# Second layer of a two-layer graph network: the base rows reach the node rows by an adding transfer on GpSimd's queue

## What is computed

```python
h = jnp.maximum(_layernorm(x, axis=-1), 0.0)                 # done by the first layer's code
w = relu(edge_length_embedded @ W_fc1 / sqrt(10)) * sqrt(2) @ W_fc2 / sqrt(100)
si0, si1 = (h0 @ W_si0, h1 @ W_si1) * a                      # "base rows", one per node
y0, y1 = (h0 @ W_l1_0, h1 @ W_l1_1) * a  gathered by edge_src
m0..m3 = products of w, y and edge_attr                      # per edge
s0..s3 = segment_sum(m0..m3, edge_dst)                       # per node
out = concat(si0 + 0.5 * (s0 @ W_l2_00 + s3 @ W_l2_10) * a, si1 + 0.5 * (...) * a)
x = x + out
```

## Time and profile before

| what | value |
|---|---|
| median of 3 runs | 2910.91 us (2899.09 to 2930.3) |
| the profiled execution | 2901.78 us, of which the span from first to last instruction is 2900.0 us |
| busy over the span | PE 91%, PEld 84%, DVE 88%, ACT 72%, POOL 61% |
| mean granted TensorE clock | 0.97 of full speed |
| chain that ended last | PE 29% of the span, an unknown queue 3%, every other part 1% or less |

### The profile page before, as it was taken

How to read it: one execution, slowest core, us unless ns; L and a number is a source line. 1 busy time by engine, 2 the same in 40 slices (tenths; PEclk the granted TensorE clock), 3 DMA queues, 4 the chain that set the end, 5 groups by cost and what they waited for, 6 DMA issues and landing times. The chain is left out here.

```text
span 2900.0 us, 93514 instructions
## 1 busy us (share of the span) xinstructions
PE 2652.8 (91%) x26822; PEld 2448.7 (84%) x26822; DVE 2546.0 (88%) x11404; ACT 2101.9 (72%) x5020; POOL 1783.5 (61%) x2035
## 2 busy tenths in 40 slices
PE   0699999999999999999999995799999999999997
PEld 0699999999999999999999994688888888888886
DVE  6799999999999999999999992587888888788886
ACT  1599999999999999999999994354455555444453
POOL 3677766776666677766676661555566555555651
PEclk9999999999999999999999997799999999899998
DMA  5244444444444444444444431455555555455552
GB/s 133 71 108 112 110 111 110 111 111 112 111 108 110 108 114 111 110 112 111 110 111 108 110 100 51 105 144 129 132 146 141 147 142 141 125 141 136 140 140 74
DMA packets 563778, 337.76 MB, mean 116 GB/s; under 512 B 220529, under 2 KB 545684, under 8 KB 563141
## 3 DMA queue, kind: packets, MB, share of 16 engines
q1 hardware_dynamic: 462033, 216.02, 29.4%
q0 software_dynamic: 48736, 83.76, 11.6%
q10 hardware_dynamic: 52500, 32.01, 3.8%
HBM read 199.48 MB, written 132.08 MB: 114 GB/s over the span
## 5 line engine op out<-in xcount | busy, mean ns | idle before, releaser
L677 POOL DMA_INDIRECT xg<-sources,win x501 | 583.8, 1165 | 489.8 <-issue 221.0
L677 POOL DMA_INDIRECT xg<-in_x,win x501 | 611.2, 1220 | 164.8 <-issue 153.2
L1140 PE MATMUL out_ps<-w_out,aggT 128*100 128x64 f32 (+2 forms) x6012 | 635.6, 256 | 9.5 <-issue 6.9
L1140 PEld LDWEIGHTS out_ps<-w_out,aggT 128*100 128x100 f32 x6012 | 607.3, 171 | 12.2 <-issue 7.5
L1128 PE MATMUL agg_ps<-sel,msg 128*128 128x100 f32 x4512 | 594.8, 282 | 6.7 <-DVE msg L824 4.5
L1128 PEld LDWEIGHTS agg_ps<-sel,msg 128*128 128x128 f32 x4512 | 544.2, 195 | 26.3 <-DVE msg L824 5.5
L967 ACT COPY xw_sb<-xw_ps 128x704 f32<-128x704 f32 (+1 forms) x502 | 307.0, 611 | 315.5 <-PE xw_ps L1116 154.0
L1116 PE MATMUL xw_ps<-w_fc,hid 65*128 65x192 f32 (+1 forms) x2004 | 461.2, 354 | 17.9 <-ACT hid L942 13.4
L986 ACT COPY aggT<-agg_ps 128x600 f32<-128x600 f32 x377 | 248.2, 658 | 150.7 <-PE agg_ps L1128 91.0
L1116 PEld LDWEIGHTS xw_ps<-w_fc,hid 65*128 65x128 f32 (+1 forms) x2004 | 322.4, 194 | 33.7 <-ACT hid L942 17.6
L950 ACT ACTIVATE hn<-xn,nmr,rs 128x192 f32<-128x192 f32 x501 | 244.4, 538 | 56.5 <-DVE nmr L772 56.5
(11 more groups left out here) (147 smaller groups left out, 5488.8 us busy)
## 6 DMA issues: line engine op xcount, KB each, us to landing
sources<-ev SPq DMA_DIRECT2D x250, 250.0 KB
xn<-in_x SPq DMA_DIRECT2D x250, 125.0 KB
xmid<-xo SPq DMA_DIRECT2D x250, 125.0 KB
xo<-xmid SPq DMA_DIRECT2D x250, 125.0 KB
xn<-sources SPq DMA_DIRECT2D x250, 125.0 KB
out<-xo ACTq DMA_DIRECT2D x250, 125.0 KB
win<-edge_rec SPq DMA_DIRECT2D x1002, 3.5 KB
ee_sb<-ee_parts SPq DMA_DIRECT2D x501, 18.0 KB
```

Of the source, the lines that this page charges most:

```text
L677: pool.indirect_dma_start(out=xg[:, t.slot, j, 0:D], out_offset=None, in_=edge_rows, in_offset=bass.IndirectOffsetOnAxis(ap=win[:, t.slot, ...
L1140: ins = pe.matmul(rows[0:NT, j, c0:c1], aggT[:, t.half, j, k, :], w[f"out{k}_"][:, :], start=fresh, stop=True, skip_group_check=not fresh)
```

## The change

The addition of the base rows leaves VectorE. GpSimd issues, for each turn, a transfer that reads the base rows from `sources` in DRAM and adds them to what stands in `xo` (`accum_op=ALU.add`). It stands in GpSimd's step behind the gathers, for turn s - 2 in step s, and waits for the landing of the node rows (`xn_in`) and for `rows_ready` of the turn four before it. SP's load of the base rows into `xn` (L626) and VectorE's `add_base` are gone. One semaphore becomes four used in turn, and a fifth for the serial pass. In the serial pass GpSimd reads the tile's number itself, adds, waits for the landing, and only then gathers.

```diff
-    base_added = None if first else sem("base_added")
+    base_added = None if first else [sem(f"base_added{k}_") for k in range(5)]
 ...
                 if (t := T(0)) and not first:
                     hold(sp, stored[t.slot], t.uses * per_store)
                     sp.dma_start(xo[0:NT, t.slot, :, 0:D], rows_of(node_rows, t)).then_inc(xn_in[t.slot], 16)
-                    sp.dma_start(xn[0:NT, t.slot, :, 0:D], rows_of(sources[:, D:2 * D], t)).then_inc(xn_in[t.slot], 16)
 ...
+            def add_base(t):
+
+                wait_apart(pool, xn_in[t.slot], (t.uses + 1) * 16, passed)
+                hold(pool, rows_ready, t.freed_m(4))
+                pool.dma_start(xo[0:NT, t.slot, :, 0:D], rows_of(sources[:, D:2 * D], t), accum_op=ALU.add).then_inc(base_added[t.n % 4], 16)
+
             def step(T):
                 if t := T(-1):
                     gather(t)
+                if (t := T(2)) and not first:
+                    add_base(t)
 ...
             def chunk(t, record, j):
+                if not first:
+                    wait_apart(pool, xn_in[t.slot], (t.uses + 1) * 16, passed)
+                    pool.dma_start(xo[0:NT, t.slot, 0, 0:D], sources[bass.ds(record * NT, NT), D:2 * D], accum_op=ALU.add
+                                   ).then_inc(base_added[4], 16)
+                    pool.wait_ge(base_added[4], (t.uses + 1) * 16)
                 gather(t)
 ...
-            def add_base(t):
-
-                b = t.tiles
-                dve.wait_ge(xn_in[t.slot], (t.uses + 1) * 32)
-                o = xo[0:NT, t.slot, 0:b, 0:D]
-                dve.tensor_tensor(o, o, xn[0:NT, t.slot, 0:b, 0:D], ALU.add).then_inc(base_added, 1)
 ...
-                    dve.wait_ge(base_added, t.m + 1)
+                    dve.wait_ge(base_added[4 if t.serial else t.n % 4], (t.uses + 1) * 16 if t.serial else (t.n // 4 + 1) * 16)
 ...
-                if (t := T(5)) and not first:
-                    add_base(t)
```

More of the change, by code:

```diff
@@ L656, in chunk @@
                 sp.dma_start(dst[0:NT, t.slot, 0, 0:D], node_rows[bass.ds(tile * NT, NT), :]).then_inc(xn_in[t.slot], 16)
-                if not first:
-                    sp.dma_start(xn[0:NT, t.slot, 0, 0:D], sources[bass.ds(tile * NT, NT), D:2 * D]).then_inc(xn_in[t.slot], 16)
             def finish(t, record, f):
@@ L710, in _, with load @@
             run_steps(step, -1)
+            def load(f):
+                return None if first else pool.value_load(long_tab[bass.ds(f, 1), 0:1], min_val=0, max_val=TILES - 1)
             def chunk(t, record, j):
+                if not first:
[3 more added lines that the diff above has]
+                    pool.wait_ge(base_added[4], (t.uses + 1) * 16)
                 gather(t)
@@ L719, in finish @@
                     rstd2(t)
-            second_pass(pool, lambda f: None, chunk, finish)
+            second_pass(pool, load, chunk, finish)
         @block.vector
@@ L925, in finish @@
                     gated_vectors(t)
-                else:
-                    add_base(t)
                 new_rows(t)
```

## The result

| | before | changed |
|---|---|---|
| median of 4 runs each | 2905.0 us (2884.29 to 2930.3) | 3036.39 us (3022.48 to 3049.85) |
| the profiled execution | 2901.78 us | 3049.85 us |

The ratio is 1.0477, with a 95% interval of 1.0393 to 1.0561: the medians lie 131 us apart, the profiled executions 148 us. The ratio leaves out the run of 2930.3 us, which was in a slow state; without it the difference of the means is 138 us.

The account below looks back on a forecast made before the run. PE bounds before; GpSimd was expected to bound the second layer after. 78 us (GpSimd) + 3 (serial pass) - 0 = 81 on 2901.8 gives 2983 us; against the median 2910.9, 2992, rounded to 2990; range 2885 to 3120.

Parts of the forecast that it names:

- This decides: Second layer, GpSimd: the added transfer lifts its turn to 4.44 us, 0.31 us above the present pace, 78 us in all.
- The takeover: Second layer: the transfer price, 0.89 us, above which GpSimd bounds instead of PE, at a pace of 4.13 us a turn.
- I take 1.2 us: GpSimd's time for one adding transfer, chosen midway between a gather's 0.95 us and 1.48 us.
- 0.95 x 200/128 = 1.48 us: GpSimd's price for the adding transfer if a gather's time goes with its rows, 200 against 128.
- 2.94 + 0.30 + 1.20: GpSimd's second-layer turn: two gathers with their gaps, a further gap, and the adding transfer; 4.44 us.
- Even doubled, they leave the DMA share of 0.55 below 0.7. Cost 0 on the path.: Second layer, DMA queues: base rows moving from SP's queue to GpSimd's, even at double cost, add 0 us.
- the special form of rival (a): Second layer: gathers held up by VectorE's addition shorten without it; GpSimd's turn 3.96 us, about 2914 us; given little, within 0.29.
- Four turns or some 15 us: Second layer, added waits: the time between the adding transfer and the use of its sum or following gathers; cost 0.
- rival (d): Second layer: late landing makes VectorE's L854 wait, 250 us more at 1 us a turn; 0.14 together with a dear transfer.
- What comes off VectorE and SP: Second layer: 250 additions of 0.481 us and 250 load issues removed, counted as 0, with at most 9 us gain.
- rival (c): Second layer: stalls shrink with less on SP's queue, 35 us won, 2876 us; sign: fewer unknown-queue rows; chance 0.10.
- The serial pass: Serial pass: the gather, now behind the node rows' landing and a whole adding transfer of about 2.6 us, comes 3 us later.

Follow-up runs that it names:

- changed, chip Q: The changed kernel, unaltered, rerun on a chip where the kernel before takes 2823.09 us without stalls; 3022.53 us, ratio 1.0715.

## Why the prediction was right in its step and short in its size

**Which engine bounds: right.** "This decides" was said of what comes onto GpSimd, and GpSimd's records and gaps fill 946 of 950 us. That alone would not show it, as they do so at PE's pace too (the plain transfer); PE's idle time and the chain, 20% POOL and 0% PE, do. The kernels with 0.848 and 1.059 us (free), 1.320, 1.552 and 1.95 us (ratios from 1.017 to 1.078) order themselves by the price as the prediction's scale says. The takeover was put at 0.89 us against the stalled pace of 4.13 us. Against PE's 3.85 us, where it should lie lower, 1.06 us was still free: the gap before the transfer that the sum contained does not exist, and the 1.171 us of a gather contained time in which it was held up.

**The price: mis-sized.** "I take 1.2 us"; it measured 1.551. The end "0.95 x 200/128 = 1.48 us" was nearer, but by chance: the price does not go with rows, as 224 rows cost 1.320. It goes with packets, and the rows that the prediction used (gathers, whose rows are joined) could not show that an added row is a packet for itself, with 120 packets of 8 bytes beside it. The Trainium skill's 1 us (DMA: Bandwidth & Descriptors, Latency and other measured facts), an estimate of +28 us in the prediction, was lower still; here 0.848 us was measured for the plain form and 1.551 for the adding one.

**The gap: too much.** GpSimd's turn was summed as 2.94 + 0.30 + 1.20. The adding transfer begins as the gather ends, and 0.30 us follow only it: 0.30 us less than summed.

**The gathers: the step that failed.** "Even doubled, they leave the DMA share of 0.55 below 0.7. Cost 0 on the path." The share is 0.63, and the cost of the added rows 2.5-fold, both near what was foreseen. But the cost on the path is not 0: the gathers grew from 1.171 to 1.291 us in the mean. The cause is not the DMA engines' load as such: with the other queues' bytes cut they are as long. The prediction had it in hand, as the special form of rival (a): gathers held up by VectorE. It gave that little on one pair of rows, where a gather starts 0.23 us before the addition and passes. But the gathers of 2 us in the earlier trace rows, which it took for an effect of catching up, end 0.83 us after VectorE's last message instruction, and the rule that it cites there from the Trainium skill (SBUF — State Buffer, Who interferes with whom) is borne out by them. What it lacked is that the new transfer, by its place and its landing, puts the next gather into the messages: 108 of 405 gathers over 1.3 us, against 91 of 460 before. Taking the addition off VectorE does not help, since the messages stay. In the kernels with an adding transfer, GpSimd's shortest turn and the number of held-up gathers give the pace, 2000 to 2700 us:

| kernel | shortest turn, us | mean turn, us | gathers over 1.3 us |
|---|---|---|---|
| changed, chip Q | 4.17 | 4.68 | 72 of 298 |
| adding 8 values | 4.17 | 4.24 | 17 of 329 |
| node rows' load narrow | 4.16 | 4.58 | 67 of 306 |
| load and store narrow | 4.18 | 4.67 | 94 of 299 |
| with the memset | 4.48 | 4.59 | 15 of 304 |
| 112 partitions | 3.92 | 4.38 | 67 of 320 |
| two transfers | 4.59 | 4.75 | 31 of 295 |

By terms, 4.44 + 0.35 (price) - 0.30 (gap) + 2 x 0.12 (gathers) = 4.73 us, for the measured 4.70. The loss of 250 x (4.70 - 4.13) = 143 us stands for the 78 that were forecast; two of the errors nearly cancel, and the gathers' growth is most of what is left.

**The waits: cost 0 as waits, with a wrong reason.** "Four turns or some 15 us" lie between the transfer and its use only while GpSimd runs ahead. VectorE's step t + 6 also makes the messages of turn t + 3, whose gathers GpSimd issues in the same step as the sum of turn t. Once GpSimd bounds, the sum is wanted as soon as it can land. So the sign that the prediction gave for rival (d), L854 waiting long for `xo<-sources`, came up, and (d) as it was meant is false all the same: with the transfer a step later nothing changed. The landing, 4.46 us after the start and not 2.6, costs time in another way, by where it puts the messages.

**What comes off VectorE and SP: worth 0, right on a chip without stalls** (the kernel without base rows, 1.0001). Where stalls occur it stays open: rival (c)'s sign, the unknown queue gone from the profile, was seen in the changed kernel too, but together with a GpSimd that bounds. A kernel without base rows, or with the plain load on GpSimd, was not run on such a chip. If the stalls went there as well, it could be worth up to 2902 - 2823 = 79 us.

**The serial pass: mis-sized.** Its chain in the changed kernel, against the earlier trace rows:

```profile
3030.55 1.79 DMA xo<-xmid
3032.59 0.57 issue
3033.16 2.60 DMA xo<-sources
3036.06 0.63 issue
3036.92 2.68 DMA xg<-sources,win
```

The landing of 2.60 us is as forecast, but the gather starts 1.16 us after it, and it was 6.4 us from the node rows' transfer to the gather's start, against 1.9 before: 4.5 us later, not 3.

**Two effects of the chip on the size.** The changed kernel takes 3022 to 3036 us on all three chips on which it, or its form with the transfer a step later, ran. The kernel before takes 2823 us where it has no stalls and about 2903 where it has them. So the same change costs 7.2% there and 4.8% here. The prediction took its base from a trace with stalls, and part of GpSimd's time was then free.

**Open.** That VectorE's messages hold the gathers up is read from where the gathers start and end, in every trace that has long ones; no kernel left the messages out or moved them alone. Why the whole adding transfer lands in 4.46 us and the narrow one in 3.20 is not separated into issue and transfer. How the gain of 112 partitions divides between the price and the held-up gathers is not separated either, and what the stalls are is not known. None of the kernels that ran beats the kernel before.

## What to carry to other kernels

Before a transfer goes to GpSimd's queue, add up that engine's time in a turn, gathers and gaps included, against the pace of the engine that bounds; here 0.85 to 1.06 us fitted, and 1.32 us cost 1.7%. Take its own time from stretches in which it catches up, since records can contain waiting: in two kernels they filled all of the time at PE's pace. An adding transfer is to be priced by its packets, each row one and more where the partitions don't divide over 16 engines: a shape of 112 partitions was cheaper than one of 100, with more rows. If an instruction whose code is unchanged gets longer, look at what ends just before it ends, many times over: a distance that is always the same, here 0.95 us behind VectorE's last message instruction, names the one that holds it up.

## What was not expected of the hardware

- An adding transfer of 200 rows occupies GpSimd for 1.552 us, a plain one for 0.848 us; with 5% of the bytes it is still 1.552 us.
- A gather on GpSimd that starts while VectorE runs TENSOR_TENSOR instructions with both inputs in SBUF can be held up until the last of them ends, and ends 0.82 us later, or 0.95 us where it follows an adding transfer; its record is just longer, up to 2.9 us.
- 224 rows over 112 partitions take 1.320 us. The price of the adding ones follows 0.76 us and 2.4 ns a packet, and 100 partitions by two bring 120 packets of 8 bytes.
- An added row of 640 bytes takes a DMA engine 74 ns, a copied one 32 ns.
- The kernel before takes 2823 us on two chips and 2902 to 2905 us on two others, with stalls in the second layer on the latter alone; with the base rows' transfer on GpSimd's queue as an adding one, no stall is in any profile.
